# A graph attention kernel: products whose results nobody reads, placed in TensorE's waits at the end of each layer

## The reference, cut to what matters

```python
xn = _layernorm(x, ln1_g[l], ln1_b[l])
pos = xn @ Wpos[l] + bpos[l] + deg[:, None] * Wdeg[l][0] + bdeg[l]
xp = xn + pos
q, k, v = (xp @ W + b for W, b in (q, k, v))          # heads of 16
att = jnp.einsum('ehd,ehd->eh', q[dst], k[src]) / scale
alpha = ex / (segment_sum(ex, dst)[dst] + 1e-16)      # ex = exp of clipped att
aggr = segment_sum(v[src] * alpha, dst)
x = x + (aggr @ Wo[l] + bo[l])
h = gelu(_layernorm(x, ln2_g[l], ln2_b[l]) @ W1[l] + b1[l])
x = x + (h @ W2[l] + b2[l])
```

## Time and profile before

| | |
|---|---|
| median of 3 runs | 2110.04 us (2108.03 to 2110.55) |
| profiled execution: its time | 2108.54 us |
| profiled execution: its span | 2106.6 us |
| TensorE busy | 1420.2 us, 67% of the span |
| VectorE busy | 1452.9 us, 69% |
| GpSimd busy | 1488.8 us, 71% |
| ScalarE busy | 914.6 us, 43% |
| mean granted TensorE clock | 0.829 of full speed |

### The profile page before, as it was taken

The page is one execution under the profiler, slowest core; times in us unless marked ns, Lnnn a source line. Parts: engine busy times, 40 slices in busy tenths (PEclk is TensorE's granted clock), DMA queues, the critical chain, the costliest instruction groups (busy, mean ns, idle before and its releaser), DMA issues.

```text
span 2106.6 us, 44014 instructions
## 1 busy us (share of the span) xinstructions
PE 1420.2 (67%) x11643; PEld 1260.0 (60%) x11644; DVE 1452.9 (69%) x2483; ACT 914.6 (43%) x1616; POOL 1488.8 (71%) x1584
## 2 busy tenths in 40 slices
PE   7667665667787777776545666666667667776664
PEld 6566655556676666665535665665556566665554
DVE  8977666666777777776557666665677767767654
ACT  4244333325465555553234333332455555455422
POOL 0277777777777777777737777777777777777773
PEclk9879889788888898987657788788999888978866
DMA  3345544555555555555424554554555555555552
GB/s 87 123 148 168 162 155 154 161 159 159 161 162 159 172 162 163 168 163 163 151 77 154 158 163 154 154 164 155 157 160 161 166 158 157 158 161 164 166 156 89
DMA packets 120301, 322.97 MB, mean 153 GB/s; under 512 B 31459, under 2 KB 43684, under 8 KB 120170
## 3 DMA queue, kind: packets, MB, share of 16 engines
q0 software_dynamic: 75072, 205.10, 32.2%
q1 hardware_dynamic: 44292, 115.07, 16.9%
q10 hardware_dynamic: 838, 1.60, 0.3%
HBM read 313.45 MB, written 9.73 MB: 153 GB/s over the span
## 4 chain that ended last, share of the span: by engine, by line
POOL 67%; issue 23%; DVE 5%; PE 3%; DMA 1%; DVEq 1%; ACT 0%; ACTq 0%; POOLq 0%; SPq 0%
POOL kv L563 67%; DVE q_parts L835 1%; DMA x<-in_x 1%; DVE qkv L922 0%; DMA kv<-kv_tab,src_idx 0%; PE ps L1335 0%; PE ps L1180 0%; DVE dots L1078 0%; DVE prod L1068 0%; DVE qkv L927 0%; DVE stats L794 0%; DVEq L356 0%; DVE msg L1102 0%; PE ps L1410 0%; PE ps L1414 0%
## 5 line engine op out<-in xcount | busy, mean ns | idle before, releaser
L563 POOL DMA_INDIRECT kv<-kv_tab,src_idx x1564 | 1485.0, 949 | 590.6 <-issue 474.6
L1335 PE MATMUL ps<-msg,hot 128*128 128x136 f32 x3896 | 657.4, 335 | 362.9 <-DVE acc L983 354.9
L1335 PEld LDWEIGHTS ps<-msg,hot 128*128 128x128 f32 x3896 | 606.0, 236 | 406.2 <-DVE msg L1102 237.6
L1320 PE MATMUL ps<-q_parts,hotT 128*128 x5844 | 472.0, 243 | 228.3 <-DVE prod L1068 178.9
L1320 PEld LDWEIGHTS ps<-q_parts,hotT 128*128 x5844 | 417.6, 109 | 295.2 <-issue 273.6
L1068 DVE TENSOR_TENSOR prod<-kv,ps 128x1024 f32<-128x1024 f32 (+1 forms) x198 | 238.7, 1205 | 272.0 <-DMA kv<-kv_tab,src_idx 246.3
L988 DVE SCALAR_TENSOR_TENSOR hot<-dst_col,neg_base,ps 128x1024 f32<-128x1024 f32 (+1 forms) x246 | 311.9, 1268 | 121.7 <-issue 118.0
L699 ACT ACTIVATE dist<-dst_rows,neg_node 128x1024 bf16<-128x1024 int32 x246 | 282.5, 1148 | 142.0 <-issue 127.4
L708 ACT ACTIVATE msg<-att 128x64 f32<-128x64 f32 (+1 forms) x198 | 49.9, 252 | 601.1 <-DVE att L1083 597.7
L702 ACT ACTIVATE hotT<-dist 128x1024 bf16 x246 | 259.9, 1057 | 47.6 <-ACT dist L699 42.0
L1078 DVE TENSOR_REDUCE dots<-prod 128x64 f32<-128x1024 f32 (+1 forms) x198 | 238.9, 1207 | 27.1 <-DVE prod L1068 19.6
(11 more groups left out here) (208 smaller groups left out, 963.4 us busy)
## 6 DMA issues: line engine op xcount, KB each, us to landing
dst_rows<-in_dst SPq DMA_DIRECT2D x194, 512.0 KB, 4.0
kv<-kv_tab,src_idx POOLq DMA_INDIRECT x1564
kv_tab<-qkv SPq DMA_DIRECT2D x25, 128.0 KB
kv_tab<-qkv SPq DMA_DIRECT2D x3, 768.0 KB, 3.8
out_tab<-z SPq DMA_DIRECT2D x24, 64.0 KB
out<-out_tab SPq DMA_DIRECT2D x1, 1498.5 KB, 8.3
hot<-in_L_gnn_W SPq DMA_DIRECT2D x2, 256.0 KB
w<-in_L_gnn_W SPq DMA_DIRECT2D x2, 256.0 KB
```

What stands on the lines that cost most here:

```text
L563: pool.indirect_dma_start(kv[:, u, c, :], None, kv_tab[l][:, :], bass.IndirectOffsetOnAxis(ap=src_idx[:, c, at(g)], axis=0)).then_inc(kv_i ...
L1320: last = MM(qd[:, c * P:(c + 1) * P], hotT[:, bass.ds(pr % 2, 1), c * P:(c + 1) * P], q_parts[:, at(t), k * D:(k + 1) * D], start=first an ...
L1335: last = MM(agg, hot[:, u % 2, c, :], msg[:, u % 2, c, :], start=(c == 0), stop=(c == nch - 1))
```

## The change

A function `spare_products(n, b)` issues n bf16 products with `zeros` as the stationary operand and the first row block of `q_parts` as the moving one, 384 columns each, into bank b. They have no semaphore, and nothing reads their result. Ten stand in group 96 and four each in groups 97 and 98, ahead of the wait for `msg_done`; in the tail six stand ahead of the first transpose of `z1`, one behind it, and, in layer 0 alone, six ahead of the transpose of `z2`. That is 31 in layer 0 and 25 in layer 1.

```diff
+                def spare_products(n, b):
+
+                    for _ in range(n):
+                        MM(bank(b, 3 * D), zeros[:, :], q_parts[:, 0, :], start=True, stop=True)
...
                     if even and runs(slot, 0):
                         transpose_ag(slot, 0, in_slot)
+                    if isinstance(g, int) and g >= NG - 3:
+                        spare_products(10 if g == NG - 3 else 4, 6)
                     pe.wait_ge(msg_done[l], g + 1)
                     sum_pair(u, g, word(d - 1)[0])
...
                 MM(in_tail["o"], agT[0], wo[:, l, :], start=False, stop=True).then_inc(o_ps[l], 1)
+                spare_products(6, 4)
                 transpose_z1(n, 0, in_tail)
+                spare_products(1, 4)
                 pe.wait_ge(z1T_done[l], n + 1)
...
                 last.then_inc(y_ps[l], 1)
+                if l < L - 1:
+                    spare_products(6, 4)
                 transpose_z2(n, 0, in_tail)
                 project_next(n, 0, in_tail)
```

## The result

The changed kernel took 2104.51 us in the median of 8 runs (2100.7 to 2106.09), before 2109.98 us in the median of 8 (2107.77 to 2110.67): 5.5 us less, ratio 0.9977 with a 95% interval of 0.9968 to 0.9986. The forecast was 2105.5 us, 4.4 us less. The single times of the changed kernel spread over 5.4 us and those of before over 2.9. For a single execution a difference of 4 us is therefore little; the medians and the profiles' own rows carry what follows.

What follows compares the result with a forecast made beforehand. GpSimd's row fetches were 67% of the chain; gains were sought at both layers' ends, where TensorE often ran at 1.2 GHz. A 4.6 us share less 0.2 charge, from 2110.04, gave 2105.5 us rounded, range 2101.8 to 2110.3.

Steps and rivals of the forecast that it cites:

- full price: Gain at both layers' ends if the high clock held throughout: layer 0 5.0 us, layer 1 3.05, together 8.0 us.
- output projection: Tail, first transpose to the sum: high clock gives back 0.75 us per layer; 0.3 of 1.5 counted.
- projection to the next layer: Layer 0's end alone: the projection takes 0.91 us instead of 1.65 at the high clock, 0.74 back.
- last groups: Between `prod` of groups 97 and 98: 1.0 us back in layer 0, 0 in layer 1; 0.9 counted.
- hidden stretch: Tail, hidden products to second sum: 4.84 us falls to 2.73, bounded by ScalarE; 2.5 of 4.2 counted.
- share: Part of the high-clock gain expected at both ends: 0.9 + 0.45 + 0.2 + 2.5 + 0.55 = 4.6 us.
- charge: Cost of spare products in TensorE's waits: 0.2 us, as sixes, singles and the ten fit their idle times.
- Rival 1: The clock is high through both tails; gain 6.5 to 8.0 us, about 2102.5; chance 0.15.
- Rival 2: Products don't raise the clock where it counts (zeros inactive, or rise too late); gain 0 to 2.5 us; chance 0.26.
- Rival 3: Slower: unhidden weight loads add 0.108 us per spare product, clock stays low; 4.5 us lost, 2114.5; chance 0.04.

Runs made afterwards that it cites:

- e3: Changed kernel with all spare products cut to 16 columns instead of 384; median 0.8 us below before, ratio 0.9997.
- e7: Changed kernel with all spare products on one row of the array instead of 128, still 384 columns; median 0.3 us below before, ratio 0.9998.
- e6: Changed kernel with the ten moved right behind the gather and six more right behind the last sum, ahead of register loads; median 7.2 us below before, ratio 0.9976.
- e9: The kernel of e6 run again for its time; median 6.8 us below before, ratio 0.9981.
- e12: The kernel of e6 run a third time; median 10.4 us below before, ratio 0.9970.
- e5: The changed kernel run again unmodified, as yardstick beside e6; median 6.8 us below before, ratio 0.9965.
- e10: The changed kernel run again unmodified, beside e9; median 0.4 us below before, ratio 0.9997.
- e8: Changed kernel with a block of q_parts instead of zeros as the stationary operand; median 2.5 us below before, ratio 1.0001.

## Why the prediction was right

**Forecast and size.** 4.4 us less was forecast; 5.5 us less in the medians, 4.9 us by the ratio, and the ends of three profiles give 4.0 against the one profile of before. Where the rest of the 5.5 was made isn't known; it is within what single profiles and medians leave open. The mechanism, the granted clock over TensorE's share of the chain, is shown by e3 and e7, where it goes when the work of the array goes, and by e6, where the full price comes out.

**The full price** of 8.0 us was right: 8.0 to 8.1 in e6, e9 and e12. The output projection gives 0.74 (0.75 predicted), the projection to the next layer 1.65 - 0.91 = 0.74, the last groups 4.76 - 3.73 = 1.03 (1.0). The hidden stretch at the high clock was put at 2.73 us and is 2.70, but that is luck. The prediction took ScalarE's row of 1.65 us for the speed of four Gelus, so that ScalarE would bound the stretch. The row was TensorE's pace at the low clock: in e6 the same four take 1.14 us. What bounds the stretch at the high clock is still TensorE, which works from 1658.61 to 1661.27 us with no idle time in between.

**The share** was right in sum and wrong in its parts. Over the six tails of the changed kernel's profiles, the hidden stretch gave back 1.37, 0, 0, 0, 1.91 and 1.23 us, 0.75 in the mean, where 1.26 was counted. The output projection gave 0.74, 0.09, 0.74, 0.74, 0.74 and 0, 0.51 in the mean, where 0.225 was counted. I had reasoned that the clock would be low at the tail's start and come up within it. In five of the six it was still high from the groups when the tail began, and in four it fell within 1.7 us behind the first transpose. Over both layers the hidden stretches brought 1.0 us less than counted and the output projections 0.6 more, so that one error made up for over half of the other. That the sum came out within 0.4 us of the forecast is in part luck.

**The charge** of 0.2 us was about right in total but for the wrong reason. The six products fit (the z transpose 1.97 us behind the sum in every profile, at either clock). The ten began 0.6 to 1.8 us behind the end of the gather in the three profiles, and where the clock was high by then this cost nothing (both layers of e5). It cost where they also ran at the low clock: the sum of 3.25 us against 4.01 left the late start out. The delay of the sum of group 96 was 0.4 us in layer 0 of the first profile after, once the 0.24 by which VectorE was later there is taken off, without lengthening the step behind it, and 0.7 in layer 1 of e10, where the step between the last `prod` rows was 4.16 us and so 0.4 of it was lost for good.

**Rival 1** (both tails high) did not occur in the three profiles; it takes e6's placement. **Rival 2** happened to single tails, not to the kernel: layer 1 of the first profile and both of e5 have the hidden stretch at 4.84. By zeros it is refuted in size (e8); by one-row products e7 bears out that they don't raise the clock. The Trainium skill's rule (TensorE: Matmul & The Clock Gate, section "Why this matters for your kernels"), by which it is idle gaps longer than any in these tails that cost the clock, is not what the runs show: in e7 the clock was high from 1656.9 us, fell at 1660.3 with TensorE busy for 2.99 us of the 3.30 before, and stayed low through the 13.72 busy us of the tail. **Rival 3** needed a product over 0.33 us. Four more take 3.38 - 2.10 = 1.28 us at the low clock in e7, 0.32 each, and 1.80 - 1.14 = 0.66 at the high one, 0.165 each (the ten of layer 1 in the row below, the six of layer 0). That agrees with the same page's section "Back-to-back issue gap".

```profile
2077.13 1.80 PE L1278 MATMUL ps<-q_parts,zeros 128*128 128x384 bf16 x10 [1.16 <-issue]
```

The stretches of e7 around the fall (PE busy, granted clock, DMA share, GB/s):

```profile
1656.90:1660.20 3.30, 2.99 (x20) 1.00 0.03 7
1660.30:1662.50 2.20, 0.59 (x4) 0.50 0.00 0
```

## What to carry to other kernels

Where a chain of short dependent steps runs at the low clock, price first what each of TensorE's steps on it would take at the high clock, from rows of the same kernel; here it gave the full gain to a tenth, against one profile of before. Before another engine (here ScalarE's Gelus) is taken as the bound, look whether its row was itself waiting for TensorE between its instructions: then it gets shorter with the clock. In this kernel the filler products held the clock through both tails when the stretch ahead of the tail, in which VectorE works, was filled too. Products on one row of the array did nothing for it and those on 128 did; nothing between was tried. Put them ahead of register loads and branches: behind them they began up to 1.8 us late and held up what they were to help. Compare the scatter and the stages of several profiles, since a placement that leaves holes gets a different share of the clock in each execution.

## What was not expected of the hardware

One row of the array against 128, at the same duration of each product, decides whether the clock rises: 13.72 us of busy time in 14.20 left it at 1.2 GHz (e7), while e6 kept 2.4 GHz for 20.40 us with TensorE busy for 15.32 and 13.94 of them. Register loads and a loop's branches in TensorE's program held back products that wait for nothing, by 0.6 to 1.8 us in the three profiles of the changed kernel; in e6, ahead of them, the same ten followed the gather at once.

On some chips the whole program took 3189 to 3244 us instead of 2110. In the profiles of e5, e9, e10 and e12 GpSimd is busy for the same time as before (1488 to 1489 us), VectorE for about the same (1444 to 1446, 1453 before), and TensorE for more (1660 to 1687, 1420 before), at a mean granted clock of 0.69 to 0.71 instead of 0.83. The waits of the changed kernel in e10 (engine and instruction, what it waited for, us in total, times, longest) show VectorE waiting for something that the profile doesn't name, at the place where it waits for fetched rows; before, the same wait was 246.3 us by the fetches' DMA. Why the program is slower there is open.

```profile
DVE prod L1068 <- remote: 441.1, 42, 16.7
```
